# Dealing the positional query rows over eight places of a score block instead of four

## The reference

```python
x = x + 0.5 * tanh(layernorm(x) @ W @ A1 @ A2 + bias)
q, k, v = (16 heads of 16 features from layernorm(x) * ln_g + ln_b, with weights and biases)
p = sinusoidal_pe @ Wp                              # (1024, 16 heads, 16)
content = (q + u_bias) @ k.T                        # per batch and head: 1024 x 1024
pos = relative_shift((q + v_bias) @ p.T)            # per batch and head: 1024 x 1024
attn = softmax((content + pos) / 4)
x = x + (attn @ v) @ Wo + bo
x = x + 0.5 * tanh(layernorm(x) @ W @ A1 @ A2 + bias)
```

## Time and profile before

| what | value |
|---|---|
| time of the kernel, median of 3 runs | 3496.66 us (3495.27 to 3497.78) |
| time of the profiled execution | 3495.08 us |
| span of the profiled execution, first to last instruction | 3493.3 us |
| front, attention, closing in that span | about 0 to 302, 302 to 3329, 3329 to 3493 us |
| TensorE busy | 91% |
| ScalarE, VectorE, GpSimd busy | 65%, 49%, 38% |
| DMA traffic | 1231 MB, mean 352 GB/s |

### The profile page before, as it was taken

One profiled execution on the slowest core, in us unless ns is written; L12 is line 12 of the kernel. 1 busy time (PEld: TensorE's weight loads), 2 busy tenths in 40 slices (PEclk: granted clock), 3 DMA queues, 4 the chain that ended last, 5 costly groups with the idle time before them and its releaser, 6 DMA issues. The chain is left out here.

```text
span 3493.3 us, 104304 instructions
## 1 busy us (share of the span) xinstructions
PE 3161.6 (91%) x34876; PEld 1962.4 (56%) x34876; DVE 1710.6 (49%) x3603; ACT 2275.2 (65%) x3255; POOL 1329.0 (38%) x1341
## 2 busy tenths in 40 slices
PE   8996999999999999999999999999999999999988
PEld 5662555555555555555555555555555555555577
DVE  7771444444444444444444444444444444444457
ACT  3432777777777777777777767777777777777633
POOL 2211444444444444444444444444444444444410
PEclk9996999999999999999999999999999999999999
DMA  5977999999999999999999999999999999999862
GB/s 164 297 247 249 378 381 378 380 377 383 379 374 382 382 378 378 381 378 382 378 381 379 376 381 382 380 378 378 380 381 377 380 381 379 380 374 384 330 193 97
DMA packets 433552, 1231.26 MB, mean 352 GB/s; under 512 B 48992, under 2 KB 133472, under 8 KB 433504
## 3 DMA queue, kind: packets, MB, share of 16 engines
q1 hardware_dynamic: 430000, 1229.12, 95.8%
q10 hardware_dynamic: 3504, 1.53, 0.2%
HBM read 617.04 MB, written 613.43 MB: 352 GB/s over the span
## 5 line engine op out<-in xcount | busy, mean ns | idle before, releaser
L818 DVE CUSTOM_DVE_ANT_0 at_pos_in<-at_ps_con,at_pos_in 128x1024 f32<-128x1024 f32 x1024 | 1253.7, 1224 | 1622.0 <-PE at_ps_con L705 1184.8
L855 POOL TENSOR_SCALAR at_pos_in<-at_pos_in,at_neg_max 128x1024 f32<-128x1024 f32 x1024 | 1147.9, 1121 | 1721.8 <-DVE at_neg_max L818 1721.8
L786 ACT ACTIVATE at_pos_out<-at_ps_pos 128x1024 f32<-128x1024 f32 x1024 | 1049.6, 1025 | 652.9 <-PE at_ps_pos L705 652.9
L705 PE MATMUL at_ps_con<-at_right,at_left 32*128 32x512 f32 x4096 | 1157.6, 641 | 262.3 <-DVE at_neg_max L818 261.1
L795 ACT ACTIVATE at_prob<-at_ps_turn 128x512 f32<-128x512 f32 x2048 | 1108.8, 596 | 277.6 <-PE at_ps_turn L729 277.6
L705 PE MATMUL at_ps_pos<-at_right,at_left 32*128 32x512 f32 x4096 | 1165.2, 645 | 28.5 <-DMA at_left<-scratch_queries 20.7
L729 PE MATMUL at_ps_turn<-keep_ident,at_pos_in 128*128 128x128 f32 x8192 | 1105.0, 278 | 0.6 <-ACT at_prob L795 0.6
L729 PEld LDWEIGHTS at_ps_turn<-keep_ident,at_pos_in 128*128 128x128 f32 x8192 | 889.8, 141 | 299.0 <-ACT at_prob L795 188.1
L741 PEld LDWEIGHTS at_ps_pv<-at_prob,at_v_aug 128*32 128x32 f32 x16384 | 416.1, 109 | 387.8 <-issue 246.7
L705 PEld LDWEIGHTS at_ps_con<-at_right,at_left 32*128 32x128 f32 x4096 | 309.5, 183 | 471.3 <-ACT at_pos_out L786 367.2
L741 PE MATMUL at_ps_pv<-at_prob,at_v_aug 128*32 128x128 f32 x16384 | 553.2, 276 | 0.8 <-issue 0.8
(11 more groups left out here) (90 smaller groups left out, 1295.8 us busy)
## 6 DMA issues: line engine op xcount, KB each, us to landing
scratch_scores<-at_pos_out SPq DMA_DIRECT2D x1024, 512.0 KB, 6.1
at_pos_in<-scratch_scores SPq DMA_DIRECT2D x1024, 512.0 KB, 6.4
scratch_queries<-fr_qk SPq DMA_DIRECT2D x128, 256.0 KB, 3.9
at_left<-scratch_queries SPq DMA_DIRECT2D x127, 256.0 KB, 6.0
fr_x<-in_L_attn_x_dram SPq DMA_DIRECT2D x16, 512.0 KB, 6.9
scratch_x<-fr_x_bo SPq DMA_DIRECT2D x16, 512.0 KB, 4.8
scratch_keys<-fr_qk SPq DMA_DIRECT2D x32, 256.0 KB, 4.9
scratch_values<-fr_values SPq DMA_DIRECT2D x8, 1024.0 KB, 5.8
```

What stands on the lines that cost most here:

```text
L705: ins = pe.matmul(banks[:, n, :], left[side][rows, t.i * P:(t.i + 1) * P], right[side][rows, :], start=True, stop=True)
L786: act.activation(pos_out[:, t.slot, :], ps_pos[:, :, :].rearrange("p a m -> p (a m)"), ACT.Copy)\
L818: dve.tensor_tensor_reduce(pos_in[:, t.slot, :], ps_con[:, :, :].rearrange("p a m -> p (a m)"), pos_in[:, t.slot, :], -SCALE, 3.0e38, ALU. ...
L855: pool.tensor_scalar(pos_in[:, t.slot, :], pos_in[:, t.slot, :], -1.0, neg_max[:, t.slot:t.slot + 1], ALU.mult, ALU.add).then_inc(shifted, 1)
```

## The change

One constant. The dealt copies of L382 and the write of L651 both follow it.

```diff
-WRITE_GAPS, READ_GAPS = 4, 1
+WRITE_GAPS, READ_GAPS = 8, 1
```

## The result

The change made the kernel slower: 3563.06 us median of 4 runs (3554.41 to 3588.18) against 3496.17 (3495.27 to 3497.78), a ratio of 1.0204, 95% interval 1.0174 to 1.0234. I had forecast no change, 3496.5 with a range of 3488 to 3514, and was wrong. On a second chip the same kernel, timed again, lost less: 3517.10 (10 runs) against 3497.16 (13 runs), 1.0049 [1.0027, 1.0071]. All shown rows of after are from the first, with a span of 3556.7 us.

The account below looks back on a forecast made before the run. The prediction took the loop as bound by the TensorE-VectorE handshake and by TensorE, not by transfers. Parts (a), (b) and (c) summed to 0 + 0 + 0, giving 3496.5 us, range 3488 to 3514.

Parts of the forecast that it names:

- What bounds the kernel: Loop steps of 2.7 us held by the handshake and 3.1 us where TensorE is full; compute does not feel transfers.
- the handshake: In the loop, content scores on TensorE, VectorE's 1.22 us, then content scores again: a step of 2.67 us.
- Part (a), the value taken for the write: Loop's write of a tile in new row order: unchanged at 1.26 us, taken from lone writes at four places.
- my upper bound of 0.52: Most the loop's write could lengthen, to 1.78 us, from the front's query writes at 294 GB/s.
- The nearest row: Profile row used to price the write: 128 rows of 4,096 bytes written alone at four places, 1.26 us.
- Part (a), the spare time: Per loop step, 2.68 us of transfer in 2.92, leaving about 0.24 us; a write lengthening by less costs 0.
- Part (b): The front's 32 dealt copies: change taken as 0, bounds 16 us less or more on ScalarE, hidden either way.
- Part (c), SyncE's issue at 0: Read-backs, waits, ring sizes and SyncE's issue of 0.52 us a write, under 1.06 us waiting a step: unchanged, 0.
- The allowance of 9.4 and 10.1 us: Loop time from a write's issue to its read-back, 9.4 us, and from read-back issue to VectorE's use, 10.1.
- Rival 1: Write places or 16 neighbouring rows collide in memory, DMA becomes the bound: slower, 3558 to 3783 us; chance 0.12.
- the padding rule of the Trainium skill: Copies with large power-of-two row distances fall to half or a quarter, 192 bytes padding not mending; a write 2.53 us.
- the markers that I named for the rival: SyncE waiting for `scratch_scores`, landings of 9 us and more, loop rate below 373 to 386 GB/s.

Follow-up runs that it names:

- experiment 9: Kernel before plus one more DMA each step, 16 rows of 4,096 bytes (64 KB) read into an unused tile: 3683.44 us, ratio 1.0498.
- experiment 5: Each write to eight places split into two DMAs of 16 x 4 rows, upper places first, front dealing for four: 3496.45 us against 3497.16 before.
- experiment 2: Kernel before with only the front's query copies dealt for eight places, the write still to four: 3504.34 us, ratio 1.0009.
- experiment 6: The change with rows of 1008 instead of 1024 numbers written, or rows 4,356 instead of 4,100 bytes apart: single runs of 3505.81 and 3573.06 us.
- experiment 7: Plain row order without relative shift, gaps forcing writes and read-backs into 16 x 8 or 32 x 4: 3726.68 and 3495.64 us, against 3495.62 before.
- experiment 10: Kernel before with each write in two DMAs of 64 neighbouring partitions, 3596.13 us; or WRITE_GAPS = 16, walked as 8 x 16 rows, 4789.14 us.
- experiment 4: Kernel before with fewer places: WRITE_GAPS, READ_GAPS = 2, 1 gave 3505.11 us, ratio 1.0020; 1, 1 gave 3838.08 us, 1.1007.
- experiment 8: Kernel before with READ_GAPS = 8, WRITE_GAPS = 4: read-backs and stores of the heads walked as 16 x 8 rows; 3756.13 us, ratio 1.0737.
- the halves: Kernel before with each write in two DMAs of 64 neighbouring partitions, 16 x 4 rows each: 3596.13 us, a single run.

## Why the prediction was wrong

**What bounds the kernel: right as far as it went.** The loop was held by the handshake and by TensorE, and the compute felt nothing of the transfers. What I drew from it was wrong. Equal busy times at unequal rates show that no transfer was late; they do not show how near it was.

**Part (a), the value taken for the write: the step that failed.** I took "the same 128 rows of 4,096 bytes written alone at four places: no change, 1.26 us". Measured: 2.14 instead of 1.43 us from first to last packet, 0.71 more, above my upper bound of 0.52, and the landing of a lone write came at 4.5 us instead of 4.0. The nearest row was nearest in size and pattern, but it was walked as 32 x 4. And I saw the fall of the outer size from 32 to 16, asked of it only whether fewer engines take part, and was content with a row that shows 16 engines busy at 294 GB/s. Busy is not fast. The same row could have been read the other way.

**Part (a), the spare time: wrong.** The 0.24 us a step was worked out from lone rates. Sixteen more rows, 0.16 us, cost 0.18 a step (experiment 9), so the mixture of reads and writes had used it up. The DMA share of 1.02 in the earlier trace rows hinted at it, and I gave it as support for a rival instead of using it in the sum. The earlier trace rows said it too: the 410 GB/s that I took for a read-back hold for the first nine slices or so. The 21 slices until the last transfers thin out have a mean of 375 GB/s, at which the 1,106 KB of a step take 2.95 us, all of the step's 2.92. Had lone costs added up, though, 0.71 less 0.24 would have been 0.47 a step and 481 us; it was 0.06, 60 us. And in experiment 5 a lone write took 0.5 us more, over twice my limit of 0.24, and the one run of it lost nothing. A lone cost sits at the start of a transfer, and in the loop something else is in flight then; that this is why it mostly vanishes is argued, not shown. Neither sum of lone rates gives the loop.

**Part (b): right.** Four copies took 3.31 us before and 3.29 after, and in experiment 2 the time stays within its noise. The step of 8 numbers costs as much as that of 4.

```profile
110.27 3.29 ACT L382 ACTIVATE fr_qk<-fr_ps_qk,keep_b_qk 128x512 f32<-128x512 f32 x4
```

**Part (c), SyncE's issue at 0: wrong, and this is the path by which the loop lost its time.** I counted the issues but not that one can be held up: 1.31 us of issuing a step became 2.23, and the 1.06 us of waiting that I set against it fell to 0.18. The allowance of 9.4 and 10.1 us between issue and need was right; it starts at the issue, and the issue came late.

**Rival 1** had the direction right, and by chance the size (3558 at 0.06 a step, the profiled run took 3558.49), for a reason that the runs refute. That the numbers meet is luck: it priced 0.30 us more for a write, and 0.71 were measured. Its places in DRAM and its neighbouring rows have no part in a lone write: experiments 6 and 7 moved them all. So the padding rule of the Trainium skill ("DMA: Bandwidth & Descriptors", section "Latency and other measured facts") was the wrong rule to weigh: at these distances no run shows it. Another rule of the same page bears on the case, section "Why a DMA increments its semaphore by 16 and not by 1": the slowest dimensions of both sides set how many engines share a transfer. The case agrees: 8 x 16 goes by eight engines (experiment 10), and the change's 16 x 8 by all 16. They are busy, and still the write is slow; a count of 16 engines was not the question. Of the markers that I named for the rival, the rate in the loop fell (372 GB/s), but SyncE's wait for `scratch_scores` was 1.3 us in all and the longest landing 9.5; both came in full in experiments 4, 8 and 9.

**Open.** What an outer size of 16 does at the start of a transfer. Why the write's issue is stretched beside read-backs of 128 plain rows in the change and the halves, and not in experiment 5, and whether that holds back the DMA engines or they it: their share is 1.02 before and after. Why the loss is 2.0% on one chip and 0.5% on another. The chips do differ without the change: with the same forms as in the kernel before, experiment 2's loop has landings of 5.0, 7.4 and 10.2 us (min, median, max) where before's has 4.6, 6.2 and 8.1, and 9 of its read-backs are late. And why plain order on both sides costs 10% as 128 rows with the shift and nothing as 32 x 4 without it; order, form and shift were not taken apart there.

## What to carry to other kernels

When a change reorders a DMA, write down the form of both access patterns before and after, outer size first, and compare with a transfer of the same form, not of the same size; here the form decided and the addresses did not. A DMA share at 1.0 while no engine waits can mean, as here, that there is no spare time: test it with one small extra transfer before pricing a change by lone rates. Look for a stretch where the transfer runs alone; four lone writes told in one line what four noisy medians could not. And watch the issuing queue as an engine of its own: when it stops waiting, it has become the bound.

## What the runs showed of the hardware

- 128 rows of 4,096 bytes written from on-chip memory to DRAM, alone: 1.43 us walked as 128, 64 x 2 or 32 x 4; 2.14 to 2.17 us as 16 x 8, in both row orders, with rows 4,100 or 4,356 bytes apart, and with shorter rows; 1.93 and 2.05 us as two of 16 x 4; not done before the next came, 3.2 us later, as 8 x 16. Read back to back with no write beside them: about 375 GB/s as 128 rows, 244 as 16 x 8.
- 8 x 16 rows against 128 partitions go by eight DMA engines: 8 packets of 4 bytes at the end of each write instead of 16, and about half of the engines busy.
- Reads and writes mixed came to 379 GB/s over this loop, at a DMA share of 1.02; with 64 KB more a step it was 377.
- An issue on SyncE's queue takes 0.32 us for a write of 128 plain rows and 0.52 to 0.55 for 32 x 4 or 16 x 8 where nothing holds it up (medians), and was held for up to 2.96 us.
- The kernel before, with its DMA share of 1.02, had runs up to 3527.93 us on one chip (19 runs) and none above 3497.13 on another (7 runs).
